# Cross-attention: the loops of ScalarE, VectorE and TensorE over the 32 iterations written out as straight programs

## What is computed

```python
q = (layernorm(x) @ Wq + bq).reshape(B, L, 16, 32)
k = (ctx @ Wk + bk).reshape(B, S, 16, 32)
v = (ctx @ Wv + bv).reshape(B, S, 16, 32)
scores = einsum('blhe,bshe->bhls', q, k)
A = softmax(scores / sqrt(32), axis=-1)
out = einsum('bhls,bshd->blhd', A, v).reshape(B, L, 512) @ Wo + bo
```

## Time and profile before

| what | us |
|---|---|
| median of 3 runs (lowest to highest) | 2742.92 (2741.66 to 2747.49) |
| the profiled execution | 2731.94 |
| its span, on which all rows stand | 2730.2 |
| from the first copy of sums (iteration 1) to the last (iteration 31), 30 iterations | 1797.0 |
| TensorE, VectorE, ScalarE busy in the span | 94%, 80%, 69% |

### The profile page before, as it was taken

The page is one execution under the profiler, slowest core; times in us unless marked ns, Lnnn a source line. Parts: engine busy times, 40 slices in busy tenths (PEclk is TensorE's granted clock), DMA queues, the critical chain, the costliest instruction groups (busy, mean ns, idle before and its releaser), DMA issues. The chain is left out here.

```text
span 2730.2 us, 43246 instructions
## 1 busy us (share of the span) xinstructions
PE 2554.0 (94%) x14123; PEld 1326.0 (49%) x14123; DVE 2195.0 (80%) x1810; ACT 1880.2 (69%) x2173; POOL 495.5 (18%) x548
## 2 busy tenths in 40 slices
PE   9999399999999999998999999999999987969998
PEld 7878134334343343333433433334334336858776
DVE  4377399989899899898998998989989975657565
ACT  3123288888788788887887888878878864523333
POOL 2113101101001010010010100101101014415664
PEclk9999699999999999999999999999989998969999
DMA  7445941111151111115111111411111017824373
GB/s 250 158 163 204 188 124 28 32 25 36 25 114 34 26 31 31 31 25 120 26 28 25 32 33 28 102 44 26 27 26 31 25 63 263 302 67 131 124 225 126
DMA packets 132923, 232.05 MB, mean 85 GB/s; under 512 B 23634, under 2 KB 56922, under 8 KB 131940
## 3 DMA queue, kind: packets, MB, share of 16 engines
q1 hardware_dynamic: 110468, 177.57, 23.1%
q0 software_dynamic: 22240, 51.68, 6.2%
HBM read 155.32 MB, written 91.66 MB: 90 GB/s over the span
## 5 line engine op out<-in xcount | busy, mean ns | idle before, releaser
L1022 ACT ACTIVATE probs<-psum 128x1024 f32<-128x1024 f32 x1664 | 1566.7, 1037 | 301.0 <-PE psum L1137 205.2
L1074 DVE TENSOR_TENSOR sums<-sums,probs 128x2048 f32<-128x2048 f32 x704 | 1646.6, 2339 | 116.1 <-ACT probs L1022 94.6
L1137 PE MATMUL psum<-q_st,k_st 97*128 97x512 f32 x3328 | 1005.4, 426 | 92.7 <-ACT probs L1022 53.4
L1137 PEld LDWEIGHTS psum<-q_st,k_st 97*128 97x128 f32 x3328 | 572.6, 191 | 755.1 <-ACT probs L1022 630.0
L1149 PE MATMUL psum<-probs,v_st 128*32 128x512 f32 x6656 | 846.3, 608 | 7.9 <-ACT probs L1022 7.9
L1149 PEld LDWEIGHTS psum<-probs,v_st 128*32 128x32 f32 x6656 | 159.2, 109 | 382.8 <-issue 295.0
L1848 PE MATMUL psum<-we_hi,wo 128*128 x624 | 218.6, 411 | 5.5 <-issue 5.1
L730 POOL DMA_DIRECT2D sum_scratch<-shared_rows x32 | 18.9, 591 | 1062.4 <-ACT shared_rows L988 1061.9
L1074 DVE TENSOR_TENSOR sums<-probs 128x2048 f32<-128x2048 f32 x32 | 73.4, 2293 | 82.4 <-ACT probs L1022 82.4
L1701 ACT ACTIVATE wo<-psum 128x512 fp32r<-128x512 f32 x78 | 46.6, 597 | 129.3 <-PE psum L1834 129.2
L1848 PEld LDWEIGHTS psum<-we_hi,wo 128*128 128x128 f32 x624 | 119.0, 191 | 31.6 <-issue 6.1
(11 more groups left out here) (197 smaller groups left out, 2041.4 us busy)
## 6 DMA issues: line engine op xcount, KB each, us to landing
q_st<-qh_scratch SPq DMA_DIRECT2D x64, 256.0 KB
token_rows<-rows SPq DMA_DIRECT2D x8, 1040.0 KB, 5.2
xn<-in_x SPq DMA_DIRECT2D x16, 512.0 KB, 6.7
qh_scratch<-o_hi SPq DMA_DIRECT2D x8, 1024.0 KB, 4.5
ql_scratch<-o_lo SPq DMA_DIRECT2D x8, 1024.0 KB, 7.7
q_st<-ql_scratch SPq DMA_DIRECT2D x32, 256.0 KB
token_rows<-in_x SPq DMA_DIRECT2D x1, 8192.0 KB, 33.3
shared_rows<-inv_scratch POOLq DMA_DIRECT2D x128, 64.0 KB, 2.2
```

The lines of the kernel that those rows point to most:

```text
L1022: nc.scalar.activation(probs[:, p_slot[t], 2 * half:2 * half + 2, :], psum[:, 2 * slot:2 * slot + 2, :], ACT.Exp, scale=SCALE).then_inc(ex ...
L1074: nc.vector.tensor_tensor(sums[b][:], a[:], probs[:, p_slot[t]], ALU.add).then_inc(added, 1)
L1137: mm = nc.tensor.matmul(psum[:, 2 * slot + h % 2, :], k_st[:, h, t * P:(t + 1) * P], q_st[:, b, h, :], start=True, stop=True)
```

## The change

The loops of the three engines are replaced by Python loops, so every iteration is its own piece of program. What each engine computes, and in which order, stays. Numbers in waits become constants, the register instructions and the branches are gone, and the programs are longer. GpSimd and SyncE aren't touched. Lines after the edits move up by a few (L1022 becomes L1020, L1074 becomes L1068, L1137 and L1149 become L1129 and L1141).

```diff
@@ attention @@
-    ROUND = 2 * S_RING
-    MIDDLE = (NIT - 2) // ROUND * ROUND
@@ ScalarE @@
-                step(0, 0)
-                with act.Fori(0, MIDDLE // S_RING) as r:
-                    for u in range(S_RING):
-                        step(r * S_RING + (u + 1), (u + 1) % S_RING)
-                for it in range(MIDDLE + 1, NIT):
+                for it in range(NIT):
                     step(it, it % S_RING)
                 fetch(NIT - 1)
@@ VectorE @@
                 dve.wait_ge(wo_lo_ready, 1)
-                with dve.Fori(0, NIT // 2 - 1) as i:
-                    step(i * 2 + 1, 1)
-                    step(i * 2 + 2, 0)
-                step(NIT - 1, 1)
+                for it in range(1, NIT):
+                    step(it, it % 2)
@@ TensorE @@
-                step(0, 0, 0, 0)
-                with pe.Fori(0, MIDDLE // ROUND) as r:
-                    for u in range(1, ROUND + 1):
-                        step(r * ROUND + u, u, r * S_RING + u // 2, r * S_RING + (u + 1) // 2)
-                for it in range(MIDDLE + 1, NIT):
+                for it in range(NIT):
                     step(it, it, it // 2, (it + 1) // 2 if it + 1 < NIT else None)
                 sum_up(NIT - 1, 1)
```

## The result

| kernel | median us | runs, lowest to highest | profiled span |
|---|---|---|---|
| before (the three runs above and one more) | 2742.29 | 2738.0 to 2747.49 | 2730.2 |
| all three loops written out | 2636.86 | 2634.78 to 2639.68 | 2633.0 |

The ratio is 0.9615 (95% interval 0.9596 to 0.9635): 105 us less by the medians, 97 us less between the two profiled executions. The forecast was 2650 in a range of 2632 to 2678.

A forecast was written before the change was run, and what follows sets the result against it. The bound was taken to be a latency loop between TensorE and ScalarE over three PSUM slots. Terms -64 - 36 + 2 + 6 = -92 us, from the median 2742.9 to 2651, shaded to 2650; range 2632 to 2678.

The forecast's parts named there:

- Part 1: ScalarE's and TensorE's ways back in the attention: pauses for instruction fetches and TensorE's slow clock go, 64 us less.
- Part 2: ScalarE's register instructions between scores ready and exponential go, 36 us less; VectorE's adds each 0.06 us slower.
- touches: VectorE running with 0.15 us to spare a period, sometimes holding up others, tightest at ScalarE's split: 2 us in all charged.
- Part 3: TensorE's waits for new keys at the three reloads stay: 2 us each, 6 us put back, between 3 and 15.
- Part 4: Straight code comes through the instruction queues, the block ahead fetched while one runs: zero cost.
- rival 3: The 11 us between profile and median lie in the 13 pauses and all go: 2640 us; chance 0.12.
- Rival 1: VectorE becomes the bound, its period growing to 56.9 to 57.7 us: 2661 to 2685, in the middle 2675; chance 0.15.
- rival 2: Straight code stalls at instruction block ends; at 0.96 us a block +14 us, 2757 us; chance 0.04.

The follow-up runs named there:

- the loop of 15 iterations: All loops written out except ScalarE's, whose body has 15 iterations and runs twice, against the kernel before: 2681.9 us against 2736.7, ratio 0.981.
- the straight kernel: The kernel with all three loops written out, against the kernel before: 2636.86 us against 2742.29, ratio 0.9615.
- VectorE's short loop: VectorE's old loop (15 rounds of 2 iterations) put back into the straight kernel: 2633.4 us against 2731.8 before, ratio 0.9637.
- the two kernels with exchanged waits: ScalarE's wait for scores moved last onto the exponential, in the loop of 15 iterations (2641.5 us) and in the kernel before with all loops kept (2704.0 us).
- the direct repeat: The straight kernel run again beside the kernel before on one chip: 2636.1 us against 2734.3, ratio 0.9634.
- the exchanged waits on VectorE: The straight kernel with VectorE's two waits for each add in the other order: 2631.9 us against 2731.8 before, ratio 0.9635.

## Why the prediction was right

**Part 1, the ways back: 64 us, right in size and cause.** The period without a way back was taken as 57.77; the loop of 15 iterations shows 57.76. The excess was 64 us by construction. That it goes when the ways back go is shown by the straight kernel, which has none of it, and by the step from nine ways back to one (41 us). TensorE's share, where I had priced the engines together, was 15 us taken out of the kernel before, and 12.4 by the four periods with its ways back. About half of what a dear way back costs goes with the slow clock behind it, and whether the clock falls varies. My part named this second cost. VectorE's zero holds too, for the reason given: its body was short. The compare-and-branch at about 0.1 us, which I had weighed from the Trainium skill's page Advanced Engine Details and Errata, section Control Flow Timing, isn't contradicted by VectorE's short loop, where no gap over 1 us was seen, and is far from the 2 to 4 us of the long ones. (With that price my own sum gives 2650 + 61 = 2711, not 2709.)

**Part 2, the register term: 36 us, measured 34.** The mechanism is shown by the two kernels with exchanged waits: not the number of instructions, but what stands between the arrival of the scores and the exponential. VectorE's slower adds came as forecast (22.35 us for nine) and didn't reach the path. I had charged 2 us for touches; the periods (56.63 on average where I had 56.57) leave 1.8 us for the two small errors together.

**Part 3, the reloads: 6 us, measured 2 in the profiled execution** (1.8 at the first, 0.2 at the third). It is a term that varies: in the other kernels a reload cost 0 to 5 us. The wait that I thought buried at the second reload wasn't there.

**Part 4, fetching straight code: zero, right.** 114 blocks were fetched in the attention, fewer than before, and no pause shows: between the first and the last copy of sums ScalarE's longest idle time is 1.45 us and VectorE's is under 1.

**The sum** was -92 against the profiled execution and came out at -97: -64 for the ways back, -34 for the register term, +2 for the reloads and -1 outside the attention. The reloads are most of the difference.

**The median** fell by 105 us to 2636.9, below the 2642 to 2662 that I gave the forecast and near the 2640 of rival 3. The weak step was to take the median's distance to the profiled execution as fixed. It was 10.4 us before and 2.1 after. Rival 3 said that the pauses vary from run to run. The spreads (5.7 us without pauses, 11.7 and 29 with them), the clock that falls as the runs get longer, and the two costs of the same pause speak for it. But part of the 105 was the draw of four runs: in the four later sets of before, with 13, 7, 9 and 7 runs, its median was 2736.7, 2731.8, 2734.3 and 2734.3, and the direct repeat gave 98. So a part of rival 3's 11 us was the draw of runs and not the pauses. How much of the rest is chip or day stays open.

**Rival 1** fell with the exchanged waits on VectorE, **rival 2** with the straight kernel itself.

## What to carry to other kernels

Ask of a loop on an engine how long its body is before you ask how often it goes round. Going back over some 140 instructions left no gap; over 400 or more the engine stood still for 2 to 4 us each time. On VectorE, which had time to spare, that cost nothing; on ScalarE it cost 4.0 to 8.8 us with what followed. If a program must stay in a loop, a longer body goes back less often: 15 iterations in place of 3 gave 41 of the 98 us.

Where an instruction waits for several semaphores, look at which wait stands on the instruction itself. The one that comes last in time should, since everything that stands behind it is latency; here one line moved gave 30 us. In these listings waits on constants and waits on registers are placed the other way round, so the listing of the built program has to be read, not the code.

## What the runs showed of the hardware that I had not expected

- A pause of ScalarE of 3.4 to 4.0 us sometimes cost a period 4.1 us and sometimes 8.3 or more. With it goes TensorE's granted clock in the 15 to 19 us behind it, 0.89 or 0.64. Two pauses of 3.45 us in one execution had the one and the other, with 2.14 us of idle time on TensorE in both.
- Straight code needed fewer fetches than the three loops: 114 blocks against 155 over the attention. VectorE's short loop alone needed ten fewer than its straight code.
- The same add, one after the other on its own result, stands 2.33 us apart when the wait for its predecessor is on the add and 2.40 when it is on a waiting instruction ahead of it.
- Where ScalarE's way back fell among the packets of a reload of keys and values (iteration 16), its gap was 7 to 8 us in place of 4, in all six kernels that had a way back there.
